# Attention and a product-key expert FFN in one kernel: in odd FFN tiles the expert copy goes ahead of the third exp, and the output product ahead of the second head's transposes

## The reference

```python
x = x + attn(layernorm(x), w_qkv, w_proj)        # 16 sequences x 512 tokens x 128, 16 heads, window of 128
h = layernorm(x)
xn = (h - mean(h)) * rsqrt(var(h) + 1e-5) * gamma + beta          # over all tokens
q = (xn @ w_q.T)                                                  # 2 x 8 heads x 128
sim = einsum('pbnhd,hkpd->pbnhk', q, keys)                        # 32 keys per head and side
sx, sy = top_k(sim, 8)
scores, pk = top_k(sx[..., :, None] + sy[..., None, :], 8)        # 8 of 1024 experts per head
o = einsum('bnd,bnhkd->bnhk', h, key_in[idx])
o = gelu(o) * softmax(scores)
x = x + einsum('bnhk,bnhkd->bnd', o, key_out[idx])
```

## Time and profile before

| | |
|---|---|
| median of 3 runs | 1668.57 us (1667.78 to 1672.3) |
| profiled execution | 1663.86 us, span 1662.1 us |
| mean granted TensorE clock | 0.964 of full |
| busy share of the span | TensorE 89%, VectorE 89%, ScalarE 79%, GpSimd 77% |
| chain that ended last, by engine | GpSimd 21%, ScalarE 13%, VectorE 10%, issue 8%, TensorE 7% |
| FFN phase | from about 700 us to the end |
| FFN groups 1 to 14 with their neighbours, 747.5 to 1605.6 us (858.1 us) | GpSimd busy 832.1, ScalarE 808.2, VectorE 796.1, TensorE 746.1 us |

### The profile page before, as it was taken

The page is one execution under the profiler, slowest core; times in us unless marked ns, Lnnn a source line. Parts: engine busy times, 40 slices in busy tenths (PEclk is TensorE's granted clock), DMA queues, the critical chain, the costliest instruction groups (busy, mean ns, idle before and its releaser), DMA issues.

```text
span 1662.1 us, 33309 instructions
## 1 busy us (share of the span) xinstructions
PE 1474.0 (89%) x10762; PEld 1019.5 (61%) x10762; DVE 1476.8 (89%) x4616; ACT 1314.8 (79%) x1805; POOL 1271.8 (77%) x1547
## 2 busy tenths in 40 slices
PE   5899999999999999788888888888888888888877
PEld 3455555555555554366767667677676776767766
DVE  4999999999999985389999999999999999999997
ACT  1376666666666666579999999999999999999995
POOL 1165555565655555399999999999999999999992
PEclk9799999999999999989999999999999999999999
DMA  6344554444445541100000000000000000000000
GB/s 160 86 109 108 121 112 111 112 105 112 114 111 113 111 102 45 51 1 20 1 20 20 1 20 20 7 14 20 20 1 20 20 2 20 20 7 14 14 7 7
DMA packets 73630, 86.40 MB, mean 52 GB/s; under 512 B 9872, under 2 KB 63760, under 8 KB 68752
## 3 DMA queue, kind: packets, MB, share of 16 engines
q1 hardware_dynamic: 72840, 82.70, 20.5%
q10 hardware_dynamic: 616, 1.57, 0.5%
HBM read 58.30 MB, written 25.95 MB: 51 GB/s over the span
## 4 chain that ended last, share of the span: by engine, by line
POOL 21%; ACT 13%; DVE 10%; issue 8%; PE 7%; DVEq 0%; ACTq 0%; POOLq 0%
POOL SUM L861 21%; DVE W L1091 7%; ACT E L984 6%; PE WT L1158 4%; ACT L901 1%; ACT L900 1%; PE MB L1101 1%; ACT W L944 1%; PE MB L1104 1%; DVE SMALL L1037 1%; ACT SIM L894 1%; DVE M8Y L1020 1%; ACT GE L900 0%; ACT GE L905 0%; ACT GE_first L900 0%
## 5 line engine op out<-in xcount | busy, mean ns | idle before, releaser
L861 POOL TENSOR_TENSOR SUM<-SIM 128x1024 f32<-128x1024 f32 x480 | 899.7, 1931 | 30.5 <-DVE W L1091 26.5
L1158 PEld LDWEIGHTS WT<-idf,W 128*128 128x128 f32 x4096 | 478.6, 147 | 210.4 <-issue 127.6
L1091 DVE SCALAR_TENSOR_TENSOR W<-SUM,SMALL,E 128x1024 f32<-128x1024 f32 x448 | 560.5, 1280 | 43.4 <-ACT E L984 43.0
L1158 PE MATMUL WT<-idf,W 128*128 128x128 f32 x4096 | 544.8, 284 | 56.4 <-DVE CT L1071 38.0
L278 POOL TENSOR_SCALAR_AFFINE_SELECT PT<-PT 128x128 f32<-128x128 f32 (+1 forms) x1024 | 337.0, 355 | 254.3 <-ACT PT L389 220.8
L984 ACT ACTIVATE E<-SUM,NB 128x1024 f32<-128x1024 f32 x448 | 495.6, 1116 | 20.4 <-DVE W L1091 17.7
L448 DVE CUSTOM_DVE_ANT_0 SY<-SY,bandf 128x384 f32<-128x384 f32 x512 | 273.1, 573 | 0.0
L389 ACT ACTIVATE PT<-TX 128x512 f32<-128x512 f32 x256 | 153.1, 598 | 113.8 <-PE TX L583 113.6
L469 DVE TENSOR_REDUCE mx<-SX 128x2 f32<-128x512 f32 x256 | 174.3, 681 | 51.1 <-PE SX L565 51.0
L391 ACT ACTIVATE PT<-TY 128x768 f32<-128x768 f32 x256 | 207.5, 810 | 3.8
L611 PE MATMUL PV<-PT,V 128*32 128x384 f32 (+1 forms) x2048 | 165.2, 441 | 0.8 <-POOL PT L278 0.7
(11 more groups left out here) (135 smaller groups left out, 1901.2 us busy)
## 6 DMA issues: line engine op xcount, KB each, us to landing
Q<-q_parts SPq DMA_DIRECT2D x288, 64.0 KB
K<-k_parts SPq DMA_DIRECT2D x90, 192.0 KB
q_parts<-qp SPq DMA_DIRECT2D x16, 384.0 KB, 2.4
k_parts<-kp SPq DMA_DIRECT2D x15, 384.0 KB, 2.4
xin<-in_x SPq DMA_DIRECT2D x16, 256.0 KB, 3.2
xres<-in_x SPq DMA_DIRECT2D x16, 256.0 KB, 9.4
x<-X SPq DMA_DIRECT2D x16, 256.0 KB, 2.2
x2T<-X2T SPq DMA_DIRECT2D x16, 256.0 KB, 2.1
```

Source lines behind the costliest of these rows:

```text
L861: return eng.tensor_tensor(SUM[(q * FH + h) % RING][:, :].rearrange("p (i j) -> p i j", i=NK), sx, sy, ALU.add)
L1091: nc.vector.scalar_tensor_tensor(out=W[h % WRING][:, :], in0=SUM[(k * FH + h) % RING][:, :], scalar=TOP[q][:, h, TOPK - 1:TOPK], in1=E[(n ...
L1158: o = pe.matmul(WT[:, e, :], W[h % WRING][:, e * P:(e + 1) * P], ident[:, :], is_transpose=True, start=(h == 0 and e % 4 == 0), stop=(h == ...
```

## The change

Two moves in odd tiles (k = 1 and 3).

On ScalarE, the copy of expert product 2k is taken at head 2, behind the shift of head 3 and ahead of E2, where it was at head 3, behind E2. Even tiles keep it where it was. On TensorE, the output product is issued ahead of the transposes of head 1, where it was ahead of those of head 2; the waits in front of it are the same. No instruction is added or removed.

```diff
-SLOT_A, SLOT_OUT, SLOT_SIM, SLOT_B = 0, 2, 4, 6
+SLOT_A, SLOT_SIM, SLOT_B = 0, 4, 6
+SLOT_OUT = (2, 1, 2, 1)
@@ scalar, group
-                    if h == COPY_A and more:
+                    if h == COPY_A and more and k % 2 == 0:
                         if k == 0:
                             wait_pos(act, S["experts_weighted"], g * GT)
                         o_copy(g + 1, 1 - b, 2 * k)
...
                     if h == LH - 1:
                         l_shift(j, k, q)
+                        if more and k % 2:
+                            o_copy(g + 1, 1 - b, 2 * k)
@@ tensor, group
-                    if h == SLOT_OUT and real:
+                    if h == SLOT_OUT[k] and real:
```

## The result

The changed kernel takes 1674.55 us (median of 8 runs, 1673.89 to 1680.91), the kernel before 1668.17 us (median of 8, 1664.94 to 1672.3). The ratio is 1.0044 with a 95% interval of 1.0027 to 1.0061: slower, by 6.4 us. The forecast was 1674.3.

A forecast was written before the change was run, and what follows sets the result against it. The prediction took VectorE's run up to W4 in odd FFN tiles as the bound. Copy +6.8, last tile -1.1 and clock 0 summed to +5.7 us on 1668.57, giving 1674.3 us, range 1666 to 1680.

The forecast's parts named there:

- The bound: FFN odd tiles: VectorE's run up to W4 sets the pace; ScalarE's 23.8 us wait at the output copy is slack.
- (b), the copy in k=1: Copy ahead of E2 delays W2 by 0.44 us in 11 k=1 tiles and 0.48 in 4: +6.8 us.
- (b) in k=3: Copy ahead of E2 in k=3 tiles: the delay is covered by 0.07 to 0.2 us, so worth 0.
- (a) in the odd tiles: Output product about 1.1 us sooner in odd tiles of groups 0 to 14; E6 still waits for W4: 0.
- (a) in the last tile: Group 15, k=3: VectorE is not tight there, so the earlier output product gains: -1.1 us, bounds 0 to -1.4.
- (c), the clock: TensorE's pauses after each Gelu, 20 of 30 followed by a low clock: taken as unchanged, 0, range +-1.8 us.
- A (faster): Rival: the wait at the output copy is on the path, gaining up to 23.8 us, 1644.8 at best; chance 0.08.
- B (given back): Rival, no change: W2's 0.44 us are given back at the Gelu, by the clock or before CT, about 1668; chance 0.2.
- C (both odd tiles): Rival: the copy costs in k=3 as well, 5 to 7 us more, about 1680; chance 0.1.
- D: Rival: TensorE's pauses nearly all get the low clock, +4 to +6 us on top, 1679; chance 0.07.

The follow-up runs named there:

- e6: As a run (not ScalarE's exp of that name): the kernel before with BNT in k=1 moved behind E2, 1670.13 us against 1667.32, ratio 1.0008.
- e4: Both moves in the k=3 tiles alone, on the kernel before: 1666.37 us against 1667.98, ratio 0.9986.
- e5: The full change plus activation BNT in k=1 moved from ahead of the shift to behind E2: 1667.53 us against the kernel before's 1667.32, ratio 1.0007.
- e1: Only the copy ahead of E2 in odd tiles, output product left behind head 1, on the kernel before: 1676.66 us against 1667.98, ratio 1.0043.
- e3: Both moves in the k=1 tiles alone, on the kernel before: 1676.71 us against 1667.98, ratio 1.0053.
- e2: Only the output product behind head 0 in odd tiles, copy left behind E2, on the kernel before: 1672.39 us against 1667.98, ratio 1.0025.

## Why the prediction was right

The time, 1674.3 forecast and 1674.55 measured, agrees better than the terms do; they were these.

- The bound. That ScalarE waits at E6 for W4 in every odd tile, and the wait at the output copy is slack, held: 21 us were added to the wait at E6, about what the wait at the output copy lost, and in k=3, where W2 is in time, the step did not change.
- (b), the copy in k=1, forecast +6.8: +6.99 in the profile, and the same in all runs with one early copy in k=1 and BNT in its place (193.15 to 193.39 against 185.9 to 186.3). Every number of the step was met within 0.03 us: E2 at 1.50 for 1.52, W2 at 2.66, E6 at 7.39 for 7.38, the next shift 5.46 behind it. All 15 tiles now stand at 2.66, and those that had W2 at 2.18 pay 0.48, as forecast; the trace of the kernel before has five of them and ten at 2.22 to 2.23, not four and eleven, which leaves the sum at 6.8.
- (b) in k=3, forecast 0: held, and the doubled copy showed how thin the cover was.
- (a) in the odd tiles, forecast 0 and said to be free because only TensorE's own order waits for head 1. The value is right for the whole change, the reason incomplete. It holds only since the copy comes early; alone the move costs 4.7 us. The step that was missing is TensorE's idle time in front of the output product, which I took for nobody's loss. My sentence that TensorE's gap there holds nobody up was wrong twice. In the kernel before TensorE has no gap there: the output product starts right behind head 1, and the wait is ScalarE's, for TensorE. And a gap there does hold others up: TensorE has no time to spare between the output product and the end of a k=1 tile.
- (a) in the last tile, forecast -1.1: -1.1 in e4 and e5 (56.95 and 56.94 us for the last group against 58.07), -0.43 in the profile of the change, where a low-clock stretch fell on the last group from 1651 to 1654 us. Such a stretch also lies there in e1 and e3, which keep the late product: 58.76 and 58.77 us, so like against like it is -1.1 again.
- (c), the clock, forecast 0 with +-1.8: +1.5 over three steps in the profile (1.98 - 0.39 - 0.08), which goes with a low stretch in 13 of 14 steps from k=0 to 1 instead of 9 (and in 9 from k=2 to 3 instead of 10).

So the sum over the FFN phase was 5.7 and the profiled one 8.1; between them lie 1.5 of the clock, 0.7 of the last tile and 0.2 of the copy. The median moved by 6.4. The group of four tiles grew by 0.57 us where 0.44 was forecast, the difference being the clock's. The close agreement of the two medians is in part luck: the kernel before alone scattered from 1664.5 to 1675.9 over 30 runs.

Of the rivals, A (faster) fell with the waits, and e4 shows what is left of it. B (given back) fell: 0.46 us a tile passed through to the end. C (both odd tiles) fell by e3 and e4. D was right in direction and small.

The rule of the Trainium skill that was weighed ("Perfetto Trace Analysis", Optimization Strategies: keep the matrix engine busy) did not decide here. The change took away ScalarE's wait for TensorE and lost; TensorE's own waits for W grew with it, from 7.6 to 16.7 us (760 to 1650 us). Where a gap was opened on TensorE, in e2, time was lost too. So a gap of TensorE can cost here, but moving its product forward gained nothing in the tiles in which VectorE sets the pace. The Trainium skill also says on that page (Matmul Optimizations) that the matrix engine scales its power with its use, so that matmuls should run back to back. The runs with zeros agree, as far as the granted clock shows it: 10.7 us.

## What to carry to other kernels

When a wait on an engine is removed, look at the next wait on the same engine: if another engine ends that one in every tile, the first was slack. And of a step moved forward in a queue, price what it now stands in front of: here 0.48 us in front of an exp whose consumer started 0.03 to 0.08 us behind it in one kind of tile and 0.58 to 0.78 in the other, which decided between a cost and none. Try the halves of an edit together and apart, since one may pay only for the other.

## What the runs showed of the hardware

A pause of TensorE behind a Gelu (2.36 to 2.38 us in 29 of 30 cases, 1.89 in the last) was followed by a fall of the granted clock to 1.2 GHz in 20 of the 30, so pauses of one length came out both ways. With seven matmuls of zeros in it (six recorded, 1.46 us), the clock fell behind none of them. The zeros cost nothing that the profile shows: the tiles behind them take 16.25 us (k=2) and 16.95 (k=0), the shortest of the kernel without them. An addition of work to the engine that the page shows as 89% busy made the kernel 0.6% faster.

The attention phase, the same code in all of these kernels, ended up to 9 us apart between profiles (first shift at 713.35 to 722.54 us). What moves it stays open.
